# Layer 0's weights in a PSUM bank of their own, later look-ups there, and earlier look-ups in the sum stages

## The reference, cut to what matters

```
h = relu(layernorm(x))                            # x: 100000 x 64
x = x + L0(h, src, dst, edge_weight)              # 25000 edges, sorted by dst
h = relu(layernorm(x))
x = x + L1(h, row=src, col=dst)                   # three layers

L0:  delta  = proj(h)[src] - proj(h)[dst]         # 4 heads x 64
     alpha  = softmax of two kinds of logits over the edges of one dst
     out    = sum over the edges of one dst of alpha * delta     # a weighted segment sum
     return h + mean_heads(out) @ w_out

L1:  for l in 0, 1, 2:
         mask   = hard sigmoid of a small network on x[row], x[col]
         rowsum = segment_sum(mask, row);  d = clip(rowsum ** -0.5, 0, 10)
         vals   = mask * d[row] * d[col]          # d[col] has to be looked up
         x      = segment_sum(vals * x[col], row) # a segment sum
         out    = out + x
```

## Time and profile before

| | us |
|---|---|
| median of 3 runs | 3068.01 |
| lowest and highest | 3067.27, 3074.73 |
| the profiled execution, its own time | 3066.8 |
| its span, first to last instruction | 3065.0 |

### The profile page before, as it was taken

How to read it: one execution, slowest core, us unless ns; L and a number is a source line. 1 busy time by engine, 2 the same in 40 slices (tenths; PEclk the granted TensorE clock), 3 DMA queues, 4 the chain that set the end, 5 groups by cost and what they waited for, 6 DMA issues and landing times.

```text
span 3065.0 us, 30516 instructions
## 1 busy us (share of the span) xinstructions
PE 1562.0 (51%) x7612; PEld 1141.0 (37%) x7612; DVE 2225.7 (73%) x5854; ACT 1035.2 (34%) x2116; POOL 1893.2 (62%) x1896
## 2 busy tenths in 40 slices
PE   1123333334310888726666545655666656665663
PEld 0022333233200445414455433534444434444442
DVE  6748999999967878935555634668866769766775
ACT  0014444444420333413333233434443434443221
POOL 0057766665278455667777774647775537773776
PEclk9985555565555877957777766668887668886555
DMA  0023433343320111142222211333332333333443
GB/s 7 0 55 88 118 109 101 112 112 99 95 66 7 30 34 37 41 86 65 61 64 60 53 39 32 68 74 102 105 106 55 68 81 103 109 94 91 125 120 82
DMA packets 279784, 226.51 MB, mean 74 GB/s; under 512 B 161732, under 2 KB 209856, under 8 KB 279482
## 3 DMA queue, kind: packets, MB, share of 16 engines
q1 hardware_dynamic: 221113, 184.48, 21.5%
q0 software_dynamic: 58496, 40.08, 6.2%
HBM read 151.81 MB, written 84.50 MB: 77 GB/s over the span
## 4 chain that ended last, share of the span: by engine, by line
POOL 33%; DVE 25%; issue 14%; DVEq 11%; PE 10%; DMA 3%; ACT 2%; SPq 1%; ACTq 0%; POOLq 0%
POOL big L1063 13%; POOL G L1043 12%; POOL out L1070 6%; PE bank L1536 3%; DVE den L1346 2%; DVE den L408 2%; DVE den L406 2%; PE bank L966 2%; DVEq L833 2%; DVEq L385 2%; DVEq L560 2%; DVE big L1673 2%; POOL regs L1939 1%; DVE den L386 1%; DVE XC L561 1%
## 5 line engine op out<-in xcount | busy, mean ns | idle before, releaser
L1063 POOL DMA_INDIRECT big<-layer_rows,late x392 | 399.1, 1018 | 187.7 <-issue 126.4
L1939 POOL DMA_INDIRECT regs<-in_x,G x200 | 202.9, 1015 | 308.1 <-DVEq L1792 174.2
L1536 PE MATMUL bank<-regs,SQ 99*128 99x256 bf16 x1308 | 262.1, 380 | 86.4 <-ACT SQ L1439 81.8
L1948 POOL DMA_INDIRECT regs<-in_x,G x200 | 210.0, 1050 | 121.7 <-DVE G L530 63.2
L674 POOL DMA_INDIRECT x_after_layer<-big,scat_i x200 | 196.5, 982 | 132.6 <-DVE big L850 84.2
L1070 POOL DMA_INDIRECT out<-G,scat_i x196 | 194.7, 994 | 106.4 <-issue 62.1
L1043 POOL DMA_INDIRECT G<-x_after_layer,own_i x196 | 201.0, 1026 | 70.0 <-issue 60.8
L1346 DVE SCALAR_TENSOR_TENSOR den<-steps,late,bank 128x256 f32<-128x256 f32 x436 | 183.3, 477 | 81.3 <-PE bank L1536 81.1
L1043 POOL DMA_INDIRECT G<-x_after_layer,far_i x196 | 196.8, 1004 | 65.3 <-issue 65.3
L1536 PEld LDWEIGHTS bank<-regs,SQ 99*128 99x128 bf16 x1308 | 168.9, 134 | 165.2 <-ACT SQ L1439 104.1
L1031 POOL DMA_INDIRECT late<-degree_factors,late x152 | 152.1, 1000 | 98.4 <-DMA degree_factors<-den 55.2
(11 more groups left out here) (409 smaller groups left out, 5287.6 us busy)
## 6 DMA issues: line engine op xcount, KB each, us to landing
den<-in_x SPq DMA_DIRECT2D x96, 256.0 KB, 4.0
x_after_layer<-den SPq DMA_DIRECT2D x96, 256.0 KB, 2.3
regs<-x_after_layer SPq DMA_DIRECT2D x96, 256.0 KB, 2.8
out<-regs SPq DMA_DIRECT2D x96, 256.0 KB, 2.1
XC<-row_of_far_degree SPq DMA_DIRECT2D x109, 128.0 KB, 3.4
layer_rows<-TS SPq DMA_DIRECT2D x98, 128.0 KB, 1.9
regs<-sought SPq DMA_DIRECT2D x49, 196.0 KB
regs<-row_of_edge SPq DMA_DIRECT2D x75, 128.0 KB
```

Source lines behind the costliest of these rows:

```text
L1063: ahead(g, l, REVERSED, lambda u, l=l: g.indirect_dma_start(far[:, tile_of(u // C, u % C), :], None, xt_d[l - 1], bass.IndirectOffsetOnAxi ...
L1536: ins = pe.matmul(bank[2 + 2 * b + k // 2][:, (k % 2) * 256:(k % 2) * 256 + 256], OH[b][0:RB1 + 1, k * P:(k + 1) * P], TAB[0:RB1 + 1, part ...
L1939: g.indirect_dma_start(GR[:, c % DEEP, k, 0, :], None, a["x"], bass.IndirectOffsetOnAxis(ap=own0[:, c * C + k:c * C + k + 1], axis=0), bou ...
L1948: g.indirect_dma_start(GR[:, c % DEEP, k, 1, :], None, a["x"], bass.IndirectOffsetOnAxis(ap=far0[:, c * C + k:c * C + k + 1], axis=0), bou ...
```

## The change

It has four parts, all in the order or the place of work; no arithmetic is added or removed.

1. Layer 0's weights go to bank 2, which nothing else uses there (32 chunks at a time, two copies in place of four). `weigh` waits for `n_proj` no more; `renew` now always does.
2. The turned products use two banks in place of three, so part n waits for the eviction of part n - 2.
3. PE's dst look-up e is issued in PE's step 2e + 2 and no longer in step 2e.
4. In the sum stages look-up j is issued in the step of the chunk of look-up j - 2 (on SP, of look-up j - 3), which is the one whose bank it takes; PE's steps are otherwise turn_z(i), turn_back(i - 1) in place of turn_z(i - 2), turn_back(i - 3).

```diff
-        WHELD = 16
-        WUP = [bank[7 - k][:, 256:512].rearrange("p (c x) -> p c x", x=C * HEADS) for k in range(2)]
+        WHELD = 32
+        WUP = bank[2][:, :].rearrange("p (c x) -> p c x", x=C * HEADS)
...
             def weigh(c, b, j):
-                if c >= 5:
-                    v.wait_ge(signal("n_proj"), c - 4)
...
             def renew(c):
-                if c + 5 >= NCH:
-                    v.wait_ge(signal("n_proj"), c + 1)
+                v.wait_ge(signal("n_proj"), c + 1)
...
-                    if n_ >= 3:
-                        pe.wait_ge(signal("m_ev"), n_ - 2)
+                    if n_ >= 2:
+                        pe.wait_ge(signal("m_ev"), n_ - 1)
...
-            staged(NCH, [(0, turn_weighed), (1, project), (3, out_proj), (0, seek)])
+            staged(NCH, [(0, turn_weighed), (1, project), (3, out_proj), (2, seek)])
...
+        def looked_at(l, lag):
+
+            at_ = [LOOKUPS[l][j - lag] if j >= lag else 0 for j in range(len(LOOKUPS[l]))]
+            return lambda i: [j for j, step in enumerate(at_) if step == i]
...
-                    staged(NC1, [(0, lambda c: spread(c) if c > LOOKUPS[l][1] else None), (5, store)])
+                    due = looked_at(l, 3)
+                    staged(NC1, [(0, lambda i: [spread(j) for j in due(i) if j >= 2]), (5, store)])
...
-                staged(NC1, [(0, hot)] + ([(4, rows)] if l < 2 else []))
+                due = looked_at(l, 2)
+                staged(NC1, [(0, lambda i: [hot(j) for j in due(i)])] + ([(4, rows)] if l < 2 else []))
...
-                staged(NC1, [(0, bring), (2, turn_z), (3, turn_back)])
+                due = looked_at(l, 2)
+                for j in due(0):
+                    bring(j)
+                staged(NC1, [(0, lambda i: [bring(j) for j in due(i) if i]), (0, turn_z), (1, turn_back)])
```

More of the change, by code:

```diff
@@ L620, in L0_sp @@
                     seek_dst_sp(sp, c // 2 + 2)
-        WHELD = 16
-        WUP = [bank[7 - k][:, 256:512].rearrange("p (c x) -> p c x", x=C * HEADS) for k in range(2)]
-        BTc = den[:, 3200:3200 + TS16 * HEADS].rearrange("p (c k x) -> p c k x", k=2, x=C * HEADS)
+        WHELD = 32
+        WUP = bank[2][:, :].rearrange("p (c x) -> p c x", x=C * HEADS)
+        BTc = den[:, 3200:3200 + TS16 * HEADS].rearrange("p (c x) -> p c x", x=C * HEADS)
         LOOKED = range(FETCHED, NC1)
@@ L816, in weigh @@
             def weigh(c, b, j):
-                if c >= 5:
-                    v.wait_ge(signal("n_proj"), c - 4)
-                if c in (0, 1, 2 * WHELD, 2 * WHELD + 1):
-                    lo = c // 2
-                    n = min(WHELD, NCH // 2 - lo)
-                    v.tensor_copy(WUP[c % 2][:, 0:n, :], BTc[:, lo:lo + n, c % 2, :])
+                if c % WHELD == 0:
+                    n = min(WHELD, NCH - c)
+                    v.tensor_copy(WUP[:, 0:n, :], BTc[:, c:c + n, :])
                     v.drain()
@@ L826, in weigh @@
                 v.tensor_tensor(Zs[b], big1[:, tiles(c), :].unsqueeze(2).broadcast_to([P, C, HEADS, F]),
-                                bc(WUP[c % 2][:, c // 2 % WHELD, :].rearrange("p (t h) -> p t h", h=HEADS), F), ALU.mult).then_inc(signal("m_z"), 1)
+                                bc(WUP[:, c % WHELD, :].rearrange("p (t h) -> p t h", h=HEADS), F), ALU.mult).then_inc(signal("m_z"), 1)
             def scan(c):
@@ L904, in out_t @@
                     s_.wait_ge(signal("m_tp"), n_ + 1)
-                    s_.activation(ZTs[b][:, q * 512:(q + 1) * 512], bank[n_ % 3][:, :], ACT.Copy).then_inc(signal("m_ev"), 1)
+                    s_.activation(ZTs[b][:, q * 512:(q + 1) * 512], bank[n_ % 2][:, :], ACT.Copy).then_inc(signal("m_ev"), 1)
             for c in range(NCH):
@@ L953, in turn_weighed @@
                     n_ = 2 * c + q
-                    if n_ >= 3:
-                        pe.wait_ge(signal("m_ev"), n_ - 2)
+                    if n_ >= 2:
+                        pe.wait_ge(signal("m_ev"), n_ - 1)
                     for k in range(C):
-                        ins = pe.transpose(bank[n_ % 3][:, k * P:(k + 1) * P], Zs[b][:, k, 2 * q:2 * q + 2, :].rearrange("p h f -> p (h f)"), ident[:, :])
+                        ins = pe.transpose(bank[n_ % 2][:, k * P:(k + 1) * P], Zs[b][:, k, 2 * q:2 * q + 2, :].rearrange("p h f -> p (h f)"), ident[:, :])
                     ins.then_inc(signal("m_tp"), 1)
@@ L1113, in L1_sp, with spread @@
             for l in range(LAYERS):
-                def spread(c, l=l):
-                    if c not in LOOKUPS[l]:
-                        return
-                    j = LOOKUPS[l].index(c)
-                    b = j % 2
+                def spread(j, l=l):
+                    b, c = j % 2, LOOKUPS[l][j]
                     if l or j >= 2:
@@ L1135, in L1_sp @@
                     for j in range(2):
-                        spread(LOOKUPS[l][j])
+                        spread(j)
                     sp.wait_ge(signal("r_val"), l + 1)
@@ L1427, in rows, with hot @@
                     s_.activation(by_half(TS[:, b]), by_pair(bank[6 + b][:, 0:256].rearrange("p (k f) -> p k f", f=F)), ACT.Copy).then_inc(signal("q_out"), 1)
-                def hot(c, l=l):
-                    if c not in LOOKUPS[l]:
-                        return
-                    j = LOOKUPS[l].index(c)
+                def hot(j, l=l):
                     b = j % 2
@@ L1522, in L1_pe, with bring @@
                 ins.then_inc(signal("r_x"), 1)
-                def bring(c, l=l):
-                    if c not in LOOKUPS[l]:
-                        return
-                    j = LOOKUPS[l].index(c)
+                def bring(j, l=l):
                     b = j % 2
-                    if c == 0:
+                    if j == 0:
                         pe.wait_ge(signal("r_carry"), 2 * l + 2)
```

## The result

The changed kernel takes 2965.12 us (median of 4 runs, 2963.28 to 2970.25), the kernel before beside it 3067.64 (4 runs, 3063.55 to 3074.73). The ratio is 0.967, with a 95% interval of 0.9645 to 0.9688. Forecast were 2961.5 us, a range of 2946 to 2988, and faster. The profiled execution took 2963.28 us, its span 2961.5, so the span is 103.5 us shorter than before.

The account below looks back on a forecast made before the run. No engine was full: PE and DVE waited for each other, and DVE's waits lengthened the stages. Gains of 39 + 33.5 + 34 = 106.5 us off 3066.8 gave 2960.3, with the median 1.2 higher: 2961.5 us, range 2946 to 2988.

Parts of the forecast that it names:

- the ring: Weighted stage: PE pauses for the pick, restarts at lower level, brings the out projection late; DVE waits 2.57 us.
- Part 1: Weighted stage: DVE's waits before weighing and at the front go; 39 us gained, between 24 and 44.
- "3 us" for the picks: Weighted stage: taken off the gain for DVE's picks waiting on late look-ups, with 14 us if PE is always low.
- reserve of 5.4 us: Weighted stage: DVE's time from `guard` to the pick, against PE's 3.6 us at upper level or 5.7 at lower.
- front term of 5.3 us: Weighted stage: the first look-up leaves the front, saving 5.3 of the 5.7 us DVE waits behind transposes.
- the 36.5 us: Weighted stage: DVE's idle time before weighing, behind the out projection, counted as gained in full.
- Part 2: Sum stages, layers 0 and 1: earlier look-ups gain 33.5 and 34 us, after 3 off for POOL, 2 for transposes.
- (a): POOL or unseen waits take back 10 us in each sum stage, 5 in the weighted stage: 2985 us, 13%.
- (b): PE drops to the lower level in most of the three stages, gaining 64 us: 3004 us, 7%.
- (c): PE low throughout the weighted stage and bounding it, +45 us; sum stages' gain eaten by handoffs: 3110 us, 2%.
- (d): Weighted stage: out-projection wait only moves to `guard` or the pick, so Part 1 gives 5 us: 2996 us, 4%.
- (e): One or both sum stages don't gain, because transfers of ids can't follow: 3028 us, 2%.

Follow-up runs that it names:

- layer0_parts: Kernel before with the weighted stage's whole change (weights in bank 2, two banks for turned products, dst look-ups two steps later), old sum stages: 3032.19 us.
- the second group: Follow-up runs sharing one chip with runs of the kernel before, which took 3065.01 us there (median of 10 runs).
- sp_two: Changed kernel, but in layers 0 and 1 SP issues look-up ids one look-up later, in the step of look-up j - 2: 2981.01 us, ratio 0.9736.
- weights_alone: Kernel before with weights in bank 2 and turned products in two banks; look-ups and sum stages as before: 3031.91 us, ratio 0.9918.
- fill: Kernel before with a wait and 12 unused identity transposes on PE ahead of each weighted-stage look-up but the first: 3031.78 us, ratio 0.9907.
- wait_only: Kernel before with the added PE wait of fill ahead of weighted-stage look-ups, without the 12 transposes: 3067.51 us, ratio 1.0001.
- sums_alone: Kernel before with the new order in the later layers' sum stages alone, weighted stage untouched: 3003.66 us, ratio 0.9794.
- the third group: Follow-up runs sharing one chip with runs of the kernel before, which took 3065.08 us there (median of 13 runs, 3044.25 to 3075.85).

## Why the prediction was right, and where it was off

**The bound and the ring.** Right, and now shown by three things: either end of the ring, cut alone, gives the whole gain; filling the pause gives it too; the wait without the filling gives nothing. DVE with its work for a pair of 10.98 us was what remained. Not right is that PE's pause for the pick goes or splits into two of about 1.2 us: it stands ahead of the projection now, as 0.37 and 2.02 us in the pair shown.

**Part 1, 39 us forecast, 37.2 in the trace.** DVE's waits fell from 49.0 to 11.7 us, which is 37.3. The term that was mis-sized is the "3 us" for the picks: they wait 6.5 us, and 10.6 in layer0_parts. The reserve of 5.4 us up to the pick was measured from `guard`, but PE's pause now lies behind the transposes, ahead of the projection (2.02 us), and where the projection starts low (3.05 us) the look-up behind it comes late. Of the front term of 5.3 us, 4.7 came: the wait before the second weighing is 0.6. With the 36.5 us, which went whole, that is 34.7; the rest up to 37.3 came by luck, from waits that the sum didn't hold: 2.2 us ahead of the second copy of the weights (L822) are gone, 2.8 at the scan are 1.4, and 0.5 at the first weighing and 0.5 behind the issue are new. The part of the sum that I didn't see is that the two edits stand for each other. The prediction gave the moved look-up the return of PE's pause and the 5.3 us at the front; in the runs it adds nothing that can be measured on top of the weights, because it gives back at the picks what it takes at the front. And the trace's gain hangs on how long the profiled execution of before was in the slow gait: counted by the medians of the second group, the weighted stage gives 32.8 us (20 to 39 by the interval), not 37.2.

**Part 2, 33.5 and 34 us forecast, 34.6 and 34.5 in the traces.** All waits ahead of picks but the first went, as said. The reason for the 3 us taken off in layer 0 was wrong: POOL isn't late, and its wait for DVE only fell to 6.9 us. DVE is held 4.5 us by PE's transposes, in layer 0 just as in layer 1 (4.6), for which the prediction had left 2. "ACT and SP hold" was right, and sp_two shows what it rests on: the ids one look-up ahead, worth 13 us. The time for each stage was given as 124 us against 157.5 and is 126.6 against 161.2, by ends that take in the last store.

**Layer 2's sum stage, 0 forecast, 0.4 us more.** Its waits for ids are nearly those of the earlier trace rows (165.9 us in place of 165.0):

```profile
ACT SQ L1433 <- DMA XC<-row_of_far_degree: 165.9, 45, 6.9
```

**The rest of the 3 us.** Forecast were 106.5 us, the trace has 103.5. In the stages 106.3 were gained (37.2 + 34.6 + 34.5). So the sum of the three terms was right to 0.2, with errors in them that cancel, and 2.8 us were lost in the stretches between, where the forecast had nothing. What causes those I haven't tried. Two of the prediction's own signs of being wrong thus showed in small: waits of DVE ahead of the pick, and longer stages between.

**Sums that don't come out.** The ends of the three terms give 116.5 us at the most, so the low end of the range would be 2951.5 us and not 2946; Part 1's low end, with 14 us for the picks, would be 28 us and not 24; rival (a)'s 25 us give 2986.5 and not 2985. The measured 2965.12 lies within the range either way.

**The rivals.** (a), waits that take back a part, happened in small: 6.5 and 4.5 and 4.6 us, and not at POOL. (b) and (c), PE low in most of the stages, didn't: granted were 0.88 in the weighted stage and 0.80 in the sum stages. (d) falls too: of the waits for the out projection one of 1.8 us is left, at L846, and it stands in the traces of before and of weights_alone as well. (e) falls in the changed kernel, and sp_two shows a mild form of it.

**The rule on transposes.** In fill, 12 transposes of the identity in PE's pause raise the granted clock of the stretch 1095.5 to 1122.8 from 0.75 to 1.00, and the stage gets faster by all that the ring had cost. The Trainium skill, "TensorE: Matmul & The Clock Gate", Part 4 (PE-mode transpose), says that such a transpose doesn't count as busy for the clock in the way a matmul does. These runs go against it, for transposes of 128x128 f32 among other matmuls: wait_only, the same but for the transposes, stays at 0.75. The measurement decides.

## What to carry to other kernels

When a wait recurs with the same length in every round, look for the ring that it is part of, and cut it at one place; here the second cut of the same ring was worth nothing more. When a look-up that is fed through several queues is moved, look at how far each queue runs ahead of the next: moved by one step with unchanged distances, the wait showed up at the next thing in PE's queue. Sum the waits of the engine that sets the pace before and after; here they gave the gain of the weighted stage to 0.1 us (37.3 against 37.2), and that of layer 0's sum stage, whose end takes in the last store, to 2.4 (41.8 - 9.6 = 32.2 against 34.6).

## What the runs showed of the hardware

A pause of PE of 2.3 us is followed by the lower level in some rounds and not in others: in wait_only the look-up behind a pause of 2.31 us took 0.88 us at 1040.41 and 1.47 at 1063.95. Once low, the kernel before stayed low at its look-ups from 1041.17 to 1205.30 us, thirteen in a row, wait_only from 1063.95 to 1200.83, eleven, and sums_alone from 1040.64 to 1204.78, thirteen. In all three the slow gait ends just behind DVE's second copy of weights (L822, started at 1198.72, 1194.24 and 1198.19 after a wait of 2.2 us), the one place where the rhythm is shifted: PE's next pause is 2.70 us in place of 2.31, the look-up behind it is the last low one, and the one after that takes 0.88. Whether the copy is the cause wasn't tried. The length of the pause alone doesn't decide the level; what does, no run here shows. That its time scatters by 30 us from run to run (3044 to 3076 in the third group), and that of fill by 5, fits a ring that is caught earlier or later; since one execution of each kernel was profiled, this is argued and not shown. Work that nobody uses paid on PE here: 12 transposes of 1.53 us a pair bought back 2.66 us of each pair of the slow gait (13.65 to 10.99).
